# Router logits of a layer chain on one core: one product per tile of tokens, instead of one per batch and a turn back

## The reference

```python
xf = norm(x).reshape(-1, 256)          # 2048 tokens
logits = xf @ router_w                 # 256 x 8 (layer 1: 256 x 7)
top_w, top_i = jax.lax.top_k(logits, 2)
...
out = jnp.einsum('enc,ne->nc', y, combine)
```

## Time and profile before

| | |
|---|---|
| median of 3 runs | 1838.64 us (1838.21 to 1839.23) |
| the profiled execution: its own time | 1836.12 us |
| its span | 1834.0 us |
| PE busy | 1574.0 us (86% of the span) |
| PE weight loads busy | 1133.5 us (62%) |
| DVE busy | 983.9 us (54%) |
| ACT busy | 480.5 us (26%) |
| POOL busy | 378.0 us (21%) |
| mean granted TensorE clock | 0.943 of full speed |

### The profile page before, as it was taken

The page is one execution under the profiler, slowest core; times in us unless marked ns, Lnnn a source line. Parts: engine busy times, 40 slices in busy tenths (PEclk is TensorE's granted clock), DMA queues, the critical chain, the costliest instruction groups (busy, mean ns, idle before and its releaser), DMA issues. The chain is left out here.

```text
span 1834.0 us, 33644 instructions
## 1 busy us (share of the span) xinstructions
PE 1574.0 (86%) x11830; PEld 1133.5 (62%) x11830; DVE 983.9 (54%) x2509; ACT 480.5 (26%) x1041; POOL 378.0 (21%) x649
## 2 busy tenths in 40 slices
PE   4888999999968987899979899568998888999980
PEld 3664889889857743455444555345665654999970
DVE  4455334444369956666556233689885554222223
ACT  1331101111066631465621111233322331111000
POOL 0102111111042001111102343422111102222216
PEclk9998999999969999899999999879998998999995
DMA  3103989989721007234214122200000003999974
GB/s 129 47 2 126 304 296 302 302 292 303 230 61 36 2 17 192 67 107 111 57 31 167 49 79 78 72 23 12 1 1 1 2 1 113 306 319 313 315 243 137
DMA packets 163230, 240.60 MB, mean 131 GB/s; under 512 B 20144, under 2 KB 110576, under 8 KB 162992
## 3 DMA queue, kind: packets, MB, share of 16 engines
q1 hardware_dynamic: 152944, 211.33, 35.5%
q0 software_dynamic: 10176, 27.80, 5.8%
HBM read 208.93 MB, written 30.15 MB: 130 GB/s over the span
## 5 line engine op out<-in xcount | busy, mean ns | idle before, releaser
L1530 DVE TENSOR_REDUCE l1a_nm<-l1a_sc 128x1 f32<-128x512 f32 (+3 forms) x256 | 107.2, 483 | 53.6 <-PE l1a_sc L1666 53.6
L2260 PE MATMUL e0b_gp<-e0b_xT,e0b_wgu 128*128 128x128 f32 x936 | 114.9, 279 | 1.8 <-DVE e0b_hT L2330 1.3
L2260 PEld LDWEIGHTS e0b_gp<-e0b_xT,e0b_wgu 128*128 128x128 f32 x936 | 107.4, 192 | 14.5 <-issue 12.3
L2281 PE MATMUL e0b_yp<-e0b_wd,e0b_hT 128*128 128x256 f32 x468 | 115.1, 388 | 0.6 <-issue 0.6
L2311 ACT ACTIVATE e0b_sg<-e0b_gp 128x640 f32<-128x640 f32 x78 | 33.5, 481 | 285.3 <-PE e0b_gp L2260 285.3
L2281 PEld LDWEIGHTS e0b_yp<-e0b_wd,e0b_hT 128*128 128x128 f32 x468 | 82.6, 189 | 21.9 <-issue 13.9
L2260 PE MATMUL e0b_up<-e0b_xT,e0b_wgu 128*128 128x128 f32 x780 | 93.5, 275 | 0.0
L2260 PEld LDWEIGHTS e0b_up<-e0b_xT,e0b_wgu 128*128 128x128 f32 x780 | 90.2, 192 | 0.0
L2260 PE MATMUL e3b_gp<-e3b_xT,e3b_wgu 128*128 128x128 f32 x624 | 78.0, 278 | 8.4 <-DMA e3b_wgu<-in_L_ffn_W 7.5
L2260 PEld LDWEIGHTS e3b_gp<-e3b_xT,e3b_wgu 128*128 128x128 f32 x624 | 74.0, 192 | 17.0 <-DMA e3b_wgu<-in_L_ffn_W 9.1
L2415 PE MATMUL e1b_gu<-e_kgu,e1b_xT 128*128 x152 | 75.2, 617 | 4.5 <-DVE e1b_xT L2480 2.8
(11 more groups left out here) (596 smaller groups left out, 3453.6 us busy)
## 6 DMA issues: line engine op xcount, KB each, us to landing
e3b_wgu<-in_L_ffn_W SPq DMA_DIRECT2D x78, 512.0 KB, 6.0
e0b_wgu<-in_L_ffn_gate_proj SPq DMA_DIRECT2D x39, 704.0 KB, 4.6
e0b_wgu<-in_L_ffn_up_proj SPq DMA_DIRECT2D x39, 704.0 KB, 5.9
e0b_wd<-in_L_ffn_down_proj SPq DMA_DIRECT2D x39, 640.0 KB, 5.2
e3b_wd<-in_L_ffn_W SPq DMA_DIRECT2D x39, 512.0 KB, 6.6
x_rows<-xn SPq DMA_DIRECT2D x3, 2048.0 KB, 7.7
l_parts<-l1p_split SPq DMA_DIRECT2D x16, 384.0 KB, 3.1
l_stack_k<-l_parts SPq DMA_DIRECT2D x48, 128.0 KB, 2.8
```

The costliest lines, as they stand in the source:

```text
L1530: nc.vector.tensor_reduce(nm[:, g % 2, q, i:i + 1], sc[q], AX_X, ALU.max, negate=True).then_inc(max_done, 1)
L2260: last = nc.tensor.matmul(dst[:, f, :], wgu[j][:, k, at + f * P:at + (f + 1) * P], xT[j][:, k, :], start=(k == 0), stop=(k == KC - 1))
L2281: last = nc.tensor.matmul(yp[:], hT[j][0:FW[f], f, :], wd[j][0:FW[f], f, :], start=(f == 0), stop=(f == FC - 1))
```

## The change

The logits are made tile by tile. The turned tile is the stationary operand (two chunks of 128x128) and the router's 8 (or 7) columns move, so that the logits come out with the tokens on the partitions, straight into `lp`. With that the banks `lt`, the tile `lts`, DVE's four copies, two semaphores and the 16 small transposes go. The products of tile t are placed after the transposes of tile t+2, and those of the last two tiles at the end.

```diff
-                lt = [st.enter_context(nc.psum_tensor(f"{tag}_lt{j}", [E, S], F32)) for j in range(2)]
-                lts = st.enter_context(nc.sbuf_tensor(f"{tag}_lts", [E, B, S], F32))
-                lt_made, lt_copied = sem("lt_made"), sem("lt_copied")
...
-                    for b in range(B if router is not None else 0):
-                        dve.wait_ge(lt_made, b + 1)
-                        nc.vector.tensor_copy(lts[:, b, :], lt[b % 2][:]).then_inc(lt_copied, 1)
...
-                    def logits(b):
-
-                        pe.wait_ge(copied, (b + 1) * TB)
-                        if b >= 2:
-                            pe.wait_ge(lt_copied, b - 1)
+                    def logits(t):
+
+                        pe.wait_ge(copied, t + 1)
                         for k in range(KC):
-                            last = nc.tensor.matmul(lt[b % 2][:], wr[:, k, :], xnT[:, k, b * S:(b + 1) * S],
-                                                    start=(k == 0), stop=(k == KC - 1))
-                        last.then_inc(lt_made, 1)
-
-                    def turn_logits(b):
-                        pe.wait_ge(lt_copied, b + 1)
-                        for t in range(TB):
-                            nc.tensor.transpose(lp[:, b * TB + t, 0:E], lts[:, b, t * P:(t + 1) * P], ident[0:E, 0:E])
+                            nc.tensor.matmul(lp[:, t, 0:E], xnT[:, k, t * P:(t + 1) * P], wr[:, k, :], start=(k == 0),
+                                             stop=(k == KC - 1))
...
-                        if router is not None and t % TB == 1 and t > TB:
-                            logits(t // TB - 1)
+                        if router is not None and t >= 2:
+                            logits(t - 2)
                     if router is not None:
-                        logits(B - 1)
-                        for b in range(B):
-                            turn_logits(b)
+                        for t in range(T - 2, T):
+                            logits(t)
```

## The result

| | before | changed |
|---|---|---|
| median, 7 runs each | 1838.21 us (1832.56 to 1839.90) | 1848.79 us (1840.69 to 1852.49) |
| profiled execution, own time | 1836.12 us | 1847.77 us |
| its span | 1834.0 us | 1845.5 us |
| mean granted TensorE clock | 0.943 | 0.930 |

The ratio is 1.005 with a 95% interval of 1.0036 to 1.0065, so the changed kernel is 6.6 to 11.9 us slower. The forecast had the sign and the mechanism, but a loss of 18.3 us where the medians differ by 10.6: 1856.9 us against 1848.79.

What follows compares the result with a forecast made beforehand. PE's list of passes was taken to bound `normalise`. The three stages' 7.4 + 3.5 + 7.4 = +18.3 us on 1836.12 gave 1854.4, and the median's 2.5 us above that execution made it 1856.9 us, range 1845 to 1864.

Steps and rivals of the forecast that it cites:

- What bounds the stage: In `normalise`, PE is the last engine to leave, so its list of passes, 14.8 us, sets the time.
- The clock: Half clock from first transpose to block end in the first and third normalise blocks; half clock in most blocks 0.77.
- The rival that full clock holds or comes back: In each normalise block PE's steady work keeps or lifts the clock; 7.2 us faster in all, 1831.4 us; chance 0.15.
- the mixed case: One of the first and third blocks starts at full clock and the second holds it; +2.4 us, 1841.0 us; chance 0.03.
- The price of a pass: Each transpose or 8-column pass with its 128x128 load takes 0.213 us at half clock, 0.115 us at full.
- The rival with loads at their own pace: In the blocks a 128-column load takes 0.107 us at either clock; total near +0, 1838.6 us; chance 0.03.
- The sum for e0's block: First normalise block: 95 passes at 0.213 plus 0.47 make 20.7 us, so PE ends 5.9 us later.
- The late fillers in `route`: Behind the first and third blocks, the 20 fillers run late after a half clock and delay the rank product; +1.5 us each.
- a fall a third of the way in: Second normalise block: 32 passes at full clock and 64 at half, 18.0 us, ending 3.5 us later.
- the cover that I had counted: Behind the second block, PE's 3.00 us idle ahead of the third group covers a clock back late by as much.
- The sum: All three stages: 7.4 + 3.5 + 7.4 = +18.3 us on the profiled execution's 1836.12 us.

Runs made afterwards that it cites:

- e3: Not a run: the third of the three stages with a changed `normalise` block; its first transpose comes at 1508.2 us before and 1517.7 us changed.
- warm_fill: Changed kernel with 10 fillers, not 5, at the start of the three normalise blocks and one 256-column filler behind each tile's transposes; 1827.56 us, ratio 0.9952.
- warm_only: Changed kernel with 10 fillers, not 5, at the start of the three normalise blocks and nothing between the tiles; 1829.75 us, ratio 0.9956.
- only_e1: Kernel before, with the new form of the logits in the second of the three normalise blocks alone; 1835.73 us, ratio 0.9988.
- logits_last: Changed kernel with all 32 transposes first and the 64 passes of 8 columns behind them; 1842.97 us, ratio 1.0029.
- route10: Changed kernel with 10 fillers in place of 20 at the start of `route`, in two stages; 1848.32 us, ratio 1.0057.
- double: Changed kernel with each tile's products made twice, the second pair over the first; 1885.60 us, ratio 1.0262.
- warm_mid: Like warm_fill, but each tile's filler stands between the products of its two chunks, not behind the transposes; 1823.11 us, ratio 0.9917.
- old_warm10: Kernel before, with 10 fillers at the start of the three normalise blocks and nothing else; 1831.13 us, ratio 0.9969.

## Why the prediction was wrong in size, point by point

**What bounds the stage: right.** PE leaves `normalise` last, and its list sets the block, in every profile above.

**The clock: right, for e0 and e3 as foretold and shown.** Half clock from the first transpose to the end of the block, and beyond it to 4.4 us into the fillers in e0 and 3.8 in e3. warm_fill holds the clock at 1.00 with more work in the list, and the block goes from 19.2 to 11.9 us. The rival that full clock holds or comes back falls for the changed kernel, though not by much: in warm_only and only_e1 the same mix held a clock that was full for 6.9 us and longer. Part of the mixed case does occur: e0 began at 1.00 in three of the seven profiles with 5 fillers (only_e1, logits_last, route10), and e3 in none; a chance of 0.03 was low for the start of e0, though none of the changed kernel's three stages kept the clock to its end. The rule of the Trainium skill that a TensorE kept busy gets past the throttle ("TensorE: Matmul & The Clock Gate", "Why this matters for your kernels") does not hold for this list: 19.15 busy us of 19.20, all at 0.50.

**The price of a pass: right** at 0.213 us (double). The rival with loads at their own pace falls with it, since it needs 0.107 us for a load at half clock.

**The sum for e0's block: the first step that failed.** "95 x 0.213 + 0.47 for the last result to land = 20.7 us". Measured 19.15. A tile has 6 passes but takes 1.17 us, 5.5 times 0.213. The rows of e0 show where: the four thin passes take 0.71 us (139.44 to 140.15) where four at 0.213 make 0.85, and the two transposes 0.46 us (140.15 to 140.61) where two make 0.43. My reading is that at the switch from transposes to products one load runs partly beside a pass that moves 128 columns; warm_mid, which added a second such place and gained what this gives, supports it. I had let every load stand in line, after a row (similarity products) that has no such switch. The price of this is 16 x 0.5 x 0.213 = 1.7 us, in e0 and again in e3: +4.3 and +4.4 in the place of +5.9.

**The late fillers in `route`: right.** "I take +1.5": the count came 7.9 and 7.6 us behind the block, and 6.3 before, so +1.6 and +1.3; route10 takes them back.

**e1: the second step that failed.** "I take a fall a third of the way in ... +3.5". The block was 3.9 us longer, near enough, but by two errors that offset each other: the clock fell after 11 passes and not after 32, and a tile paid 5.5 distances and not 6. The step that failed is what comes behind the block, which the sum has at no change: the count came only 1.0 us later, because the way from the block to the count was 2.9 us shorter. That way is the store of `xn`, ACT's wait for it, and PE's third and fourth groups of the shared expert. First the kernel before, then the changed one, then only_e1:

```profile
968.72 0.37 SPq L1981 DMA_DIRECT2D x_rows<-xn  x1
977.73 1.09 ACT L1885 ACTIVATE xn<-e1s_gp 128x512 f32<-128x512 f32 x2 [6.11 <-DMA x_rows<-xn]
...
981.05 0.37 SPq L1966 DMA_DIRECT2D x_rows<-xn  x1
981.10 5.39 PE L1837 MATMUL e1s_gp<-xnT,e1s_wg 128*128 128x512 f32 x8 [0.30 <-PEq L312]
986.33 3.60 PE L1837 MATMUL e1s_up<-xnT,e1s_wu 128*128 128x512 f32 x8
988.62 1.09 ACT L1870 ACTIVATE xn<-e1s_gp 128x512 f32<-128x512 f32 x2 [4.66 <-DMA x_rows<-xn]
989.76 3.69 PE L1837 MATMUL e1s_gp<-xnT,e1s_wg 128*128 128x512 f32 x8
...
963.25 0.37 SPq L1993 DMA_DIRECT2D x_rows<-xn  x1
970.81 1.08 ACT L1897 ACTIVATE xn<-e1s_gp 128x512 f32<-128x512 f32 x2 [4.65 <-DMA x_rows<-xn]
```

ACT began 9.0 us after the store was issued before, and 7.6 us after it now: -1.4 us. The third group ran at half clock before, behind 3.00 us in which PE was idle, 5.20 us; now it ran at full clock, 3.69 us: -1.5 us. The late clock cost only the first group (5.39 us against 3.67), and there PE has time until ACT is through. This much of the cover that I had counted was right.

The block's own delay is not covered at all, since the store is issued when the block has ended. The profiles show it (us):

| profile | form in e1 | e1's block | store issued to ACT's start | start of third group to fourth | block to count |
|---|---|---|---|---|---|
| before | old | 14.4 | 9.0 | 5.0 | 20.3 |
| old_warm10 | old | 14.4 | 8.5 | 5.2 | 20.1 |
| only_e1 | new | 10.5 | 7.6 | 3.6 | 17.6 |
| changed | new | 18.4 | 7.6 | 3.5 | 17.4 |
| double | new | 32.1 | 7.5 | 3.5 | 17.4 |

Blocks of 10.5 to 32.1 us have the count equally far behind them, 17.4 to 17.8 us in all eleven profiles with the new form, and 20.1 and 20.3 in both with the old. So the 2.9 us belong to the form of the logits, whether the clock fell or not, and not to a cover. In both old profiles PE was idle for 2.5 and 3.0 us ahead of the third group and the clock was at 0.50 for most of it; in the new ones PE was idle for at most 1.5 us and the group ran at full clock. Why the store lands earlier isn't settled. e1 cost +1.0 in all.

**The sum.** 18.3 forecast, 12.6 measured in the three stages: -1.5 and -1.7 for e0 and e3, -2.5 for e1. What remains to the median's 6.6 to 11.9 us lies in the part outside, -1.2 us between these two profiles. Over all thirteen profiles that part takes between 1752 and 1763 us, though no experiment does more in it than add fillers to PE's waits. I had taken the sum against one execution and given nothing for that, though a clock that isn't tied to the program was named among the rivals.

## What to carry to other kernels

Swapping which operand is stationary doesn't only move the work from columns to loads; it can take away what kept TensorE's clock at full: in the kernel before the clock rose inside e0 and e3 and stayed at 1.00 to the end of the block; in the changed one both stayed at 0.50, and e1 fell to it. When a product gets thin, look at the granted clock at the point where it begins, put some wide products ahead of it so that it begins at full, and place one wide, idle product among the thin ones: with both, this change went from 0.5% slower to 0.8% faster, 0.3% of which the wide products ahead give to the old form too. And before you let a wait for a transfer cover a delay, look where that transfer is issued: if it is issued behind the delay, it moves with it.

## What was not expected of the hardware

- 8-column passes behind 128x128 f32 loads stand 0.213 us apart at half clock (double), but the 6 passes of a tile take 5.5 such distances. The reading is that a load can run beside a pass that moves 128 or 256 columns and hardly beside one of 8. With one filler of 256 bf16 columns between a tile's four thin passes, a tile with 7 instructions took 0.65 us at full clock (warm_mid), less than the 0.72 us of the same 7 with the filler elsewhere (warm_fill, products of two tiles from 142.25 to 142.97).
- The same mix of passes, behind the same 5 fillers, kept a full clock for anything between 1.5 us (route10, e1) and a whole block of 10.5 us (only_e1).
- The same stretch of code between e0 and e1 took from 793.5 to 800.3 us in different profiles, with 61.4 to 78.5 us of it at half clock.
